# Softmax sums of an attention as two float32 products with a column of ones

## What is computed

```
scores  = einsum("bhqd,bhkd->bhqk", q, k)        # clipped to -80..80, causal
weights = softmax(scores / sqrt(d_qk), axis=-1)
attn    = einsum("bhqk,bhkd->bhqd", weights, v)
out     = attn.transpose(0, 2, 1, 3).reshape(B, S, H * D_H) @ W_O.T
```

## Time and profile before

| | |
|---|---|
| runs | 1306.41, 1306.52, 1306.58 us; median 1306.52 us |
| the profiled execution | 1306.28 us, of which the span of the trace 1304.4 us |
| TensorE busy | 1279.4 us, 98% of the span, 6233 matmul records |
| VectorE, ScalarE, GpSimd busy | 55%, 50%, 48% |
| granted TensorE clock | full, in all 40 slices |
| chain that ended last | PE 92% |

### The profile page before, as it was taken

One profiled execution on the slowest core, in us unless ns is written; L12 is line 12 of the kernel. 1 busy time (PEld: TensorE's weight loads), 2 busy tenths in 40 slices (PEclk: granted clock), 3 DMA queues, 4 the chain that ended last, 5 costly groups with the idle time before them and its releaser, 6 DMA issues.

```text
span 1304.4 us, 20533 instructions
## 1 busy us (share of the span) xinstructions
PE 1279.4 (98%) x6233; PEld 1047.0 (80%) x6233; DVE 722.1 (55%) x1349; ACT 648.6 (50%) x1163; POOL 626.0 (48%) x535
## 2 busy tenths in 40 slices
PE   4999999999999999999999999999999999999998
PEld 3788898888888888888887688887888888887886
DVE  6472255223222222222224788888888888888777
ACT  6411133222222222222225677777777777777775
POOL 5125566995060003300001577677667777676543
PEclk9999999999999999999999999999999999999999
DMA  9226564664251113311112243322243223323012
GB/s 299 66 98 230 212 221 122 191 183 151 66 154 58 60 55 105 109 62 58 58 49 86 75 97 66 63 47 60 48 79 50 51 54 66 63 37 67 18 50 98
DMA packets 82168, 123.34 MB, mean 95 GB/s; under 512 B 20177, under 2 KB 28497, under 8 KB 82065
## 3 DMA queue, kind: packets, MB, share of 16 engines
q1 hardware_dynamic: 48912, 56.43, 15.5%
q0 software_dynamic: 11312, 27.23, 9.6%
q10 hardware_dynamic: 21840, 38.36, 9.1%
HBM read 74.41 MB, written 39.05 MB: 87 GB/s over the span
## 4 chain that ended last, share of the span: by engine, by line
PE 92%; POOL 2%; DVE 2%; issue 1%; DMA 1%; ACT 1%; SPq 0%; ACTq 0%; POOLq 0%; DVEq 0%
PE bank L49 86%; PE bank L1505 2%; PE bank L1446 2%; PE bank L1588 1%; DMA rot_sin<-sum_b 0%; DMA rows_a<-in_x 0%; POOL sum_b L614 0%; POOL rot_sin L583 0%; POOL slots L493 0%; POOL sum_b L611 0%; POOL rstd L488 0%; POOL rot L588 0%; POOL sum_b L616 0%; SPq L435 0%; DVE stats L945 0%
## 5 line engine op out<-in xcount | busy, mean ns | idle before, releaser
L49 PE MATMUL bank<-store_b,store_a 128*128 128x512 f32 (+1 forms) x1536 | 319.1, 359 | 3.2 <-issue 1.2
L49 PE MATMUL bank<-slots,x_turned 128*128 x1296 | 317.6, 394 | 0.3 <-DVE x_turned L969 0.3
L49 PEld LDWEIGHTS bank<-store_b,store_a 128*128 128x128 f32 x1536 | 256.1, 189 | 60.3 <-issue 8.7
L49 PEld LDWEIGHTS bank<-slots,x_turned 128*128 128x128 f32 x1296 | 239.2, 188 | 48.1 <-issue 0.7
L991 DVE TENSOR_TENSOR hid_t<-bank,hid_t 128x512 fp32r<-128x512 f32 x70 | 48.4, 691 | 342.2 <-ACT hid_t L682 342.2
L49 PE MATMUL bank<-slots,hid_t 128*128 (+1 forms) x840 | 208.4, 397 | 0.0
L49 PE MATMUL bank<-store_b 128*128 128x512 f32 x768 | 180.1, 390 | 0.1
L49 PEld LDWEIGHTS bank<-slots,hid_t 128*128 128x128 f32 x840 | 153.7, 188 | 30.9 <-DVE hid_t L991 0.2
L49 PEld LDWEIGHTS bank<-store_b 128*128 128x128 f32 x768 | 143.8, 188 | 31.1 <-issue 0.9
L1342 DVE TENSOR_TENSOR store_b<-p_store,store_b 128x512 fp32r<-128x512 f32 x128 | 137.0, 1073 | 26.9 <-ACT store_b L863 26.8
L676 ACT ACTIVATE hidden<-bank 128x512 f32<-128x512 f32 x70 | 41.8, 597 | 208.3 <-PE bank L49 208.3
(11 more groups left out here) (200 smaller groups left out, 1767.7 us busy)
## 6 DMA issues: line engine op xcount, KB each, us to landing
staging<-in_w SPq DMA_DIRECT2D x56, 256.0 KB, 2.8
sorted_y<-y_store ACTq DMA_DIRECT2D x54, 256.0 KB, 2.0
rows<-sorted_x ACTq DMA_DIRECT2D x51, 260.0 KB, 2.7
rot_sin<-sum_b SPq DMA_DIRECT2D x128, 64.0 KB, 2.0
staging<-in_wg SPq DMA_DIRECT2D x28, 256.0 KB, 2.8
y_store<-in_x ACTq DMA_DIRECT2D x16, 256.0 KB, 3.4
shared_y<-y_store ACTq DMA_DIRECT2D x16, 256.0 KB, 2.2
raw<-in_wot SPq DMA_DIRECT2D x16, 256.0 KB, 2.8
```

The lines of the kernel that those rows point to most:

```text
L49: made = pe.matmul(out, a, b, start=first and n == 0, stop=last and n == len(pairs) - 1, skip_group_check=onto)
```

## The change

The six float32r products of a unit become two float32 products: one of the ones column with `prob(u, 0)`, one with `sum_b`, unrounded both. So that group 2's first piece is counted, GpSimd adds it into the second half of `prob(u, 0)` in place (two heads of 128 queries, half of the group's columns), after the low part of group 0 is taken and before `sine(u+1)`. GpSimd's subtraction for the low part of `sum_b`, ScalarE's rounding of it, and the one rounding of the ones fall away. `sum_step` now counts four steps a unit. Waits for `sums_low` and `unit_rounded` become waits for `dens_done`, `sum_step` and `unit_made`; VectorE's clip into the slot of `prob(u, 0)` waits for `dens_done`.

```diff
@@ -221,15 +221,13 @@
         o_split = carve(4 * SEQ, "down").rearrange("p (s n h t) -> p s n h t", s=2, n=2, h=2)
         p_hi = [carve(BANK, "gated", "down") for _ in range(NG)]
         p_lo = [carve(BANK, "gated", "down") for _ in range(NG)]
-        sum_b_hi, sum_b_lo = (carve(2 * H2, "down").rearrange("p (h t) -> p h t", h=2) for _ in range(2))
         m_slots = [v.rearrange("p (h s l) -> p h s l", h=2, s=2) for v in m_slots]
         v_slots = [v.rearrange("p (h s d) -> p h s d", h=2, s=2) for v in v_slots]
 
         ctx = whole.enter_context(ExitStack())
         raw = tile(ctx, "raw", [P, 2, 3 * P + D])
         raw_wr = tile(ctx, "raw_wr", [P, P])
-        unit = tile(ctx, "unit", [P, 2, 2])
-        unit_r = tile(ctx, "unit_r", [P, 2, 2], F32R)
+        unit = tile(ctx, "unit", [P, 2, 4])
         sum_store = tile(ctx, "sum_store", [P, 2, 2, 2, 2])
         inv_store = tile(ctx, "inv_store", [P, 2, 2, 2, 2])
         ratio = tile(ctx, "ratio", [P, 2, 2, 2])
@@ -356,10 +354,11 @@
                 dve.wait_ge(on["y_done"], NBK)
                 return
             v, f = divmod(n, NG)
-            dve.wait_ge(on["sum_step"], 3 * v + 3)
             if f == 0:
                 dve.wait_ge(on["p_low0"], v + 1)
+                dve.wait_ge(on["dens_done"], v + 1)
             else:
+                dve.wait_ge(on["sum_step"], 4 * v + 4)
                 dve.wait_ge(on["p_low"], (NG - 1) * v + f)
 
         def prob(u, g):
@@ -604,22 +603,24 @@
                 pool.tensor_tensor(p_lo[0], prob(u, 0), p_hi[0].bitcast(F32), ALU.subtract).then_inc(on["p_low0"], 1)
 
                 w = [prob(u, g).rearrange("p (h t) -> p h t", h=2) for g in range(NG)]
+                w1_q1 = prob(u, 2)[:, 0:2 * P].rearrange("p (h t) -> p h t", h=2)
                 w3_q3 = prob(u, 2)[:, 2 * P:4 * P].rearrange("p (h t) -> p h t", h=2)
+                pool.wait_ge(on["p_low0"], u + 1)
+                pool.wait_ge(on["exps_done"], NG * u + 3)
+                pool.tensor_tensor(w[0][:, :, P:2 * P], w[0][:, :, P:2 * P], w1_q1, ALU.add).then_inc(
+                    on["sum_step"], 1)
                 if u + 1 < NU:
                     sine(u + 1)
                 pool.wait_ge(on["exps_done"], NG * u + 4)
                 pool.tensor_tensor(sum_b[:], w[1], w[3], ALU.add).then_inc(on["sum_step"], 1)
                 pool.wait_ge(on["exps_done"], NG * u + 5)
-                pool.wait_ge(on["sum_step"], 3 * u + 1)
+                pool.wait_ge(on["sum_step"], 4 * u + 2)
                 pool.tensor_tensor(sum_b[:], sum_b[:], w[4], ALU.add).then_inc(on["sum_step"], 1)
-                pool.wait_ge(on["sum_step"], 3 * u + 2)
+                pool.wait_ge(on["sum_step"], 4 * u + 3)
                 pool.tensor_tensor(sum_b[:, :, P:2 * P], sum_b[:, :, P:2 * P], w3_q3, ALU.add).then_inc(
                     on["sum_step"], 1)
                 if u + 1 < NU:
                     rotate(u + 1)
-                pool.wait_ge(on["sums_high"], u + 1)
-                pool.tensor_tensor(sum_b_lo, sum_b[:], sum_b_hi.bitcast(F32), ALU.subtract).then_inc(
-                    on["sums_low"], 1)
                 if u >= 2 and u - 2 < NT // 2 * TOP_K:
                     n, b = divmod(u - 2, NB)
                     pool.wait_ge(on["out_added"], TB * (u - 1))
@@ -751,7 +752,7 @@
                 if u:
                     act.wait_ge(on[f"rot_swapped{(u - 1) % 2}"], 64 * ((u - 1) // 2 + 1))
                 if u >= 2:
-                    act.wait_ge(on["sums_low"], u - 1)
+                    act.wait_ge(on["dens_done"], u - 1)
                 act.activation(rot_raw, ring.bank("rotate", u), ACT.Copy).then_inc(on["rot_copied"], 1)
 
             def rotate_high(u):
@@ -882,8 +883,6 @@
                 act.activation(bank, bank, ACT.Copy, scale=ratio[:, u % 2, tt // 2, tt % 2:tt % 2 + 1]).then_inc(
                     on["rescaled"], 1)
 
-            act.wait_ge(on["unit_made"], 3)
-            act.activation(unit_r[:], unit[:], ACT.Copy).then_inc(on["unit_rounded"], 1)
             head_weights(0, 0, 0)
             head_weights(0, 1, 0)
             evict(NBK - 2)
@@ -916,8 +915,6 @@
                 if u + 1 < NU:
                     query(u + 1, 0)
                     query(u + 1, 1)
-                act.wait_ge(on["sum_step"], 3 * u + 3)
-                act.activation(sum_b_hi, sum_b[:], ACT.Copy).then_inc(on["sums_high"], 1)
                 if u + 1 < NU:
                     rotate_high(u + 1)
                 if b == 1 and p + 1 < PAIRS:
@@ -1686,15 +1683,12 @@
 
             def sums(u):
                 ring_bank_free(pe, "sums", u)
-                pe.wait_ge(on["unit_rounded"], 1)
+                pe.wait_ge(on["unit_made"], 3)
+                pe.wait_ge(on["sum_step"], 4 * u + 1)
                 row = ring.bank("sums", u)[0:2, :]
-                second_half = row.rearrange("p (h t) -> p h t", h=2)[:, :, P:2 * P]
-                product(pe, row, [(unit_r[:, 0, :], s[0]) for s in (p_hi, p_lo)], last=False)
-                product(pe, second_half, [(unit_r[:, 0, :], s[2][:, 0:2 * P].rearrange("p (h t) -> p h t", h=2))
-                                          for s in (p_hi, p_lo)], first=False, last=False)
-                pe.wait_ge(on["sums_low"], u + 1)
-                product(pe, row.rearrange("p (h t) -> p h t", h=2),
-                        [(unit_r[:, 1, :], sum_b_hi), (unit_r[:, 1, :], sum_b_lo)], first=False).then_inc(
+                pe.matmul(row, unit[:, 0, 0:2], prob(u, 0), start=True, stop=False)
+                pe.wait_ge(on["sum_step"], 4 * u + 4)
+                pe.matmul(row, unit[:, 1, 0:2], sum_b[:].rearrange("p h t -> p (h t)"), start=False, stop=True).then_inc(
                     on["dens_done"], 1)
 
             def attend(u):
```

More of the change, by code:

```diff
@@ L258, in program @@
              "scale_step", "scale_made", "y_done", "y_evicted", "cat_high", "cat_low")
-        sems("cap_filled", "cap_made", "unit_made", "unit_rounded", "proj_done", "ckv_high", "proj_taken", "kr_done",
+        sems("cap_filled", "cap_made", "unit_made", "proj_done", "ckv_high", "proj_taken", "kr_done",
              "lat_turned", "lat_high", "lat_low", "head_done", "head_high", "head_low", "wr_high", "wr_low",
@@ L262, in program @@
              "q_done", "q_high", "q_low", "scores_done", "exps_done", "clipped", "p_high", "p_low0", "p_low",
-             "sum_step", "o_done", "o_high", "o_low", "sums_high", "sums_low", "dens_done", "rows_made", "inverted",
+             "sum_step", "o_done", "o_high", "o_low", "dens_done", "rows_made", "inverted",
              "ratio_made", "part_done", "rescaled", "out_done", "out_added")
```

## The result

The changed kernel takes 1331.4 us (median of 4 runs, 1331.1 to 1332.4) against 1306.5 us of the kernel before, measured beside it: a ratio of 1.0193, 95% interval 1.018 to 1.0206. It is slower by 24.9 us; forecast were 15.6 us and a range of 1318.5 to 1326. The direction was right and the size was not: the result lies 5.4 us above the upper end.

A forecast was written before the change was run, and what follows sets the result against it. TensorE was taken to bound the kernel; 31 units x 0.55 = +17.0, unit 0 nothing, waits that go -1.4, together +15.6 us, gave 1322.0 us, range 1318.5 to 1326.

The forecast's parts named there:

- The bound: TensorE is nearly always busy, so a change in its work reaches the end nearly one to one.
- What goes, 1.16 us: The six float32r products of the sums on TensorE: five passes of 512 columns, 1.16 us a unit, no hidden wait.
- What comes, 1.71 us: Two float32 products of 512 columns at 0.85 us each, so TensorE's work grows by 0.55 us a unit.
- both of my ways to the price: Head weights' float32 products: start to next instruction 0.85 us; units with against without them, 0.86 us for 512 columns.
- Waits that go, -1.4 us: TensorE's waits for the late rotary chain after unit 0 vanish, as the chain gets 0.55 us more room a unit.
- Unit 0 free: In unit 0 TensorE stands for the rotary chain until 727.15 either way, so the edit costs and gains nothing there.
- GpSimd's addition for nothing: The new 128x256 addition, 1.27 us, fits in GpSimd's 2.11 us of idle time before the sine and costs nothing.
- rival B: GpSimd's new addition runs much slower than forecast and delays the rotary chain; at 3 us, 1331 us; chance 0.05.
- The sum, in place of 17.0 + 0 - 1.4: Forecast change: 31 units x 0.55 = +17.0, unit 0 nothing, waits that go -1.4, result +15.6 us.
- A: At the sums, a float32 product with a two-column stationary operand takes only 0.45 us: 1301.5 us; chance 0.06.
- C: The sums' float32 products cost 0.91 us each, through type changes or separate passes: 1325.6 us; chance 0.10.
- The bound of 1.02 us: Upper bound for one float32 product on TensorE: its two records with the modelled end.

The follow-up runs named there:

- e1_wide: The changed kernel with the stationary operands of both float32 products 128 columns wide in place of two: 1323.5 us.
- e5_w32: The changed kernel with the stationary operands of both float32 products 32 columns wide in place of two: 1332.2 us.
- e5_w64: The changed kernel with the stationary operands of both float32 products 64 columns wide in place of two: 1332.6 us.
- e10_w96: The changed kernel with the stationary operands of both float32 products 96 columns wide in place of two: 1323.2 us.
- e2_waits: The changed kernel with the semaphore waits of the sums moved to earlier products of attend, so that the float32 products wait for nothing: 1331.1 us.
- e3_twice: The changed kernel with ones of 0.5 and each float32 product made twice, four in a row in place of two: 1384.2 us.
- e4_one: The changed kernel with only `sum_b` in float32, the rest of the sums in four float32r products, and no new GpSimd addition: 1325.4 us.
- e7_no_add: The changed kernel without GpSimd's new addition, the first piece of group 2 left out of the sum: 1330.9 us against 1331.4.
- e11_chain: The kernel before, with VectorE starting the first rotary half's low part once ScalarE has rounded that half, not both: 1306.3 us against 1306.4.

## Why the prediction was wrong

**The bound: right.** TensorE's work decides; the change was passed on one to one.

**What goes, 1.16 us: right**, five passes with no wait in them.

**What comes, 1.71 us: right for the passes, wrong for the whole.** Two float32 products with operands of 96 or 128 columns gave a unit of 18.43, the forecast's +0.55. The step that failed is the sentence "That these had a stationary operand of 128 columns and the new ones have two should not help". I took width for something that could only help or do nothing, and had read only float32r rows for it. A float32 product with a narrow operand costs 0.28 us a unit around it, the time of its weight load and of the one behind it, which no longer run under other products; 31 units of it are 8.7 us, and 1323.5 + 8.7 = 1332.2 stands beside the measured 1331.4. e1_wide, e5_w32, e5_w64 and e10_w96 show that it is the width, e2_waits that it is not the semaphores, e3_twice that it is paid once for a row of such products, and e4_one that a row of one pays it in full.

That also explains why both of my ways to the price agreed and misled: the head weights are float32 between float32r neighbours too, but with 128 columns. A change of type costs nothing there.

**Waits that go, -1.4 us: wrong, about -0.4.** In the trace after, three units are still longer, by 0.22, 0.53 and 0.17 us, though the chain has 0.55 us more room. The longest of them:

```profile
948.88 1.29 POOL L582 TENSOR_TENSOR rot_sin<-rot_sin,sin_t 128x512 f32<-128x512 f32 x1 [3.00 <-DMA rot_sin<-sum_b]
...
958.64 1.88 PE L49 MATMUL bank<-store_b,store_a 128*128 128x512 f32 x7 [0.25 <-DVE store_b L1252]
```

GpSimd waited 3.0 us for the DMAs in place of 1.3, 1.7 us late. Such units differ from trace to trace: those of e2_waits, e7_no_add and e10_w96 have none, e1_wide has three. I had treated one execution's late units as a fixed sum that a little room would remove; that 0.55 us of it did not is what this trace shows, and e11_chain, with 0.22 us of room, gained nothing that could be measured.

**Unit 0 free: right.** TensorE reached the chain earlier and stood at it, as said, the wait longer than the 0.18 us of before:

```profile
727.82 0.73 PE L49 MATMUL bank<-store_b,store_a 128*128 128x512 f32 x2 [0.54 <-DVE store_b L1252]
```

**GpSimd's addition for nothing: right**, with a price of 0.74 us where L616 had given 1.27; rival B is out (e7_no_add).

**The sum, in place of 17.0 + 0 - 1.4:** 17.0 + 8.7 - 0.4 = 25.3 against 24.9 measured.

**The rivals.** A, a cheap narrow product, had the right place and the wrong sign: width mattered, to the worse. C had foreseen an extra cost of changing over but took its size from 0.91 us a product; measured with all gaps, a product costs 1.99 / 2 = 0.99, 0.08 more. Of its reasons, the change of type is refuted by e1_wide, and separate passes by the 0.86 us from one product to the next in e3_twice. The bound of 1.02 us that I had for a product, the end of its modelled record, would have covered the result: 31 x (2.04 - 1.16) - 1.4 = +25.9. I left it out of the range, though nothing in the trace showed the operation in its new form. The passes themselves are what the Trainium skill (FP8 and Floating Point Precision, TensorE Precision Notes) gives, four to a product: 0.428 us for each of the two records is 0.214 a pass.

## What to carry to other kernels

Price an operation from rows of its exact form, operand sizes included; where the trace has it only in another form, keep the modelled end of the record as a bound, and ask what lies between it and its neighbours, not only how long it streams. Where a float32 product of a few columns must be on a full TensorE, pad its stationary operand with zeros to 96 columns or more, if its output bank has the rows free, and look whether the weight loads start ahead of their products again. And before a wait that one late DMA causes is counted as a gain, look at the next thing that hangs on the same DMA: in e11_chain TensorE waited for that instead.

## What the runs showed of the hardware

- A float32 product with a stationary operand of 2, 32 or 64 columns is not prepared for: its first weight load starts with the product, not 0.11 us ahead (e1_wide), and the load behind a row of them starts 0.94 us after the last one's own start (1016.30 against 1015.36), with 128 columns 0.43 us after. That cost 0.28 us for each row of such products with 2 columns and 0.33 with 64, the time of the two loads; with 96 or 128 columns it cost nothing. float32r products with 2 columns have no such gap (load at 1019.54, product at 1019.66). The Trainium skill (TensorE: Matmul & The Clock Gate, "Architectural detail: the array is 16× 32×32, not 1× 128×128") says that TensorE's queue can pull weight loads ahead of products in flight; the trace agrees for every form read here but this one.
- What could lie behind the step: the Trainium skill (TensorEngine Tiling (Array Packing), Key Properties) says that changing the tiling mode drains TensorE. The Trainium skill's list of modes (TensorEngine Tiling (Array Packing), Available Configurations) has 64 and 32 columns beside 128 and nothing between. The Trainium skill (PSUM — Partial Sum Buffer, The four PSUM rules) mentions that float32r matmuls force the mask of all column groups. By these, as I read them, a float32 operand of up to 64 columns changes the mode on entering and on leaving a row of such products, one of 96 or a float32r one does not. Every width and type that ran agrees: gaps with 2, 32 and 64 columns of float32, none with 96, 128 or float32r, one pair of gaps for four products in e3_twice. That the mode is the cause is argued, not shown: no view names the mode of an instruction.
- GpSimd's addition of 128x256 took 0.74 us at its new place, and the same form as the last step of `sum_b` (L620) mostly 1.28. Its neighbour seems to set this: in the changed kernel L620 took 1.28 at 1010.81, begun beside VectorE's subtraction L1339, whose operands lie in SBUF, and 0.74 at 953.87, beside L1263, one of whose operands is a bank; the new place stands beside the clips, which read a bank. No run was made to separate it.
- VectorE is slowed in its turn: L1254, 64x512 with both inputs in SBUF, took 0.68 us in the kernel before and 1.10 in e11_chain, where it starts beside GpSimd's L621. An earlier start can so be half eaten up by a slower instruction.
